# A dense layer folded into one on-chip matrix per batch, and run in one block with the SwiGLU

## The reference

```python
x = x + attention(x, ...)       # 8 key heads of 4 query heads each, paged cache of 512 keys + 128 new ones
# the dense layer, with W (512, 512), b (512), coeff (8), mask (8, 512, 512) of 0 or 1
output = einsum('bsi,oi->bso', x, W) + b
sign   = 2 * mask - 1
diff   = einsum('bsi,bio->bso', x, sign)
x = x + output + diff * coeff[:, None, None]
x = x + swiglu(x, ...)          # W_gate, W_up (1376, 512), W_down, each with a rank-16 adapter picked by batch
x = x + einsum('bsi,boi->bso', x, L3_weight[ids])
```

## Time and profile before

| | |
|---|---|
| median of 3 runs | 1438.1 us (1436.93 to 1439.56) |
| profiled execution, its own time | 1439.11 us |
| its span, first to last instruction | 1437.3 us |
| TensorE busy | 1386.7 us, 96% of the span |
| VectorE busy | 986.5 us, 69% |
| ScalarE busy | 852.8 us, 59% |
| GpSimd busy | 675.3 us, 47% |
| granted TensorE clock, mean | 0.992 |
| moved by DMA | 163.93 MB |

### The profile page before, as it was taken

How to read it: one execution, slowest core, us unless ns; L and a number is a source line. 1 busy time by engine, 2 the same in 40 slices (tenths; PEclk the granted TensorE clock), 3 DMA queues, 4 the chain that set the end, 5 groups by cost and what they waited for, 6 DMA issues and landing times. The chain is left out here.

```text
span 1437.3 us, 25483 instructions
## 1 busy us (share of the span) xinstructions
PE 1386.7 (96%) x7864; PEld 1206.7 (84%) x7864; DVE 986.5 (69%) x2067; ACT 852.8 (59%) x2200; POOL 675.3 (47%) x965
## 2 busy tenths in 40 slices
PE   5999999999999999999999999999998869999998
PEld 4888888888888888888888888888887657888886
DVE  6777777777777777777777777777775645545544
ACT  6666665766576556666665666666554636434444
POOL 5765565555555555655565555555443550000202
PEclk9999999999999999999999999999999989999999
DMA  5354236414621462155236413621210553533422
GB/s 181 109 173 144 59 89 194 126 33 125 203 66 29 146 204 58 44 166 155 58 88 191 117 42 120 203 70 31 38 51 1 192 169 106 173 135 113 167 87 103
DMA packets 162395, 163.93 MB, mean 114 GB/s; under 512 B 121632, under 2 KB 129440, under 8 KB 152096
## 3 DMA queue, kind: packets, MB, share of 16 engines
q1 hardware_dynamic: 156384, 127.54, 30.0%
q0 software_dynamic: 5952, 35.65, 7.5%
HBM read 131.71 MB, written 31.46 MB: 114 GB/s over the span
## 5 line engine op out<-in xcount | busy, mean ns | idle before, releaser
L496 ACT ACTIVATE at_pT_hi<-at_ps 128x512 fp32r<-128x512 f32 x320 | 178.4, 600 | 173.6 <-PE at_ps L884 173.4
L422 POOL TENSOR_SCALAR at_probs<-at_probs,at_row_inv 128x640 f32<-128x640 f32 x256 | 205.6, 803 | 155.3 <-DVE at_row_inv L716 147.0
L661 DVE TENSOR_TENSOR at_pT_lo<-at_ps,at_pT_hi 128x512 fp32r<-128x512 f32 x320 | 208.5, 685 | 91.6 <-ACT at_pT_hi L496 91.6
L710 DVE CUSTOM_DVE_ANT_0 at_scores<-at_ps,at_mask,at_inv_rms 128x640 f32<-128x640 f32 x256 | 224.1, 878 | 67.9 <-PE at_ps L65 66.4
L539 ACT ACTIVATE at_probs<-at_scores,at_neg_max 128x640 f32<-128x640 f32 x256 | 213.1, 833 | 57.9 <-DVE at_neg_max L710 56.5
L63 PE MATMUL at_ps<-at_kT_hi,at_qT_hi 128*128 128x320 f32 x512 | 164.8, 322 | 0.3 <-DVE at_qT_lo L661 0.2
L884 PE MATMUL at_ps<-ident,at_probs 128*128 128x128 f32 x1280 | 160.5, 272 | 1.7 <-POOL at_probs L422 1.7
L65 PE MATMUL at_ps<-at_kT_hi,at_qT_lo 128*128 128x320 f32 x512 | 158.2, 309 | 0.0
L64 PE MATMUL at_ps<-at_kT_lo,at_qT_hi 128*128 128x320 f32 x512 | 158.0, 309 | 0.0
L884 PEld LDWEIGHTS at_ps<-ident,at_probs 128*128 128x128 f32 x1280 | 145.0, 141 | 10.8 <-POOL at_probs L422 2.4
L63 PE MATMUL at_ps<-at_pT_hi,at_v_hi 128*128 128x512 f32 x320 | 131.8, 412 | 2.1 <-DVE at_pT_lo L661 2.1
(11 more groups left out here) (211 smaller groups left out, 3496.6 us busy)
## 6 DMA issues: line engine op xcount, KB each, us to landing
kT_pages<-at_kv_stage SPq DMA_DIRECT2D x14, 1024.0 KB, 4.6
v_pages<-at_kv_stage SPq DMA_DIRECT2D x14, 1024.0 KB, 4.5
at_k_raw<-kT_pages SPq DMA_DIRECT2D x56, 256.0 KB, 3.2
at_v_raw<-v_pages SPq DMA_DIRECT2D x56, 256.0 KB, 3.9
sw_wgu_raw<-in_sw_gu SPq DMA_DIRECT2D x22, 512.0 KB, 3.3
staging<-in_L_cond_Wq SPq DMA_DIRECT2D x8, 1024.0 KB, 6.8
staging<-in_L_cond_Wo SPq DMA_DIRECT2D x8, 1024.0 KB, 5.1
ds_mask_raw<-in_mask_Bx4096x_ik SPq DMA_DIRECT2D x8, 1024.0 KB, 5.2
```

What stands on the lines that cost most here:

```text
L422: pool.tensor_scalar(probs[:, h, :], probs[:, h, :], row_inv[:, h:h + 1], 1.0, ALU.mult, ALU.mult).then_inc(probs_done, 1)
L496: act.activation(out, src, ACT.Copy).then_inc(done, 1)
L661: dve.tensor_tensor(out, src, hi_part.bitcast(F32), ALU.subtract).then_inc(done, 1)
L710: dve.tensor_tensor_reduce(out=scores[h % 2][:], in0=slot(h), in1=mask[:, b, :], scale=inv_rms[b % 2][:, h:h + 1], scalar=3.0e38, op0=ALU. ...
```

## The change

The dense layer is done with one matrix per batch, M = W^T + I + 2 coeff mask, in float32. W comes turned from the host; GpSimd adds the identity to `staging` once (`prepare_dense`); VectorE makes a quarter of a matrix per instruction, in place of the mask (`DenseWeights.weights`), ScalarE makes its high part, GpSimd three of the four rests (two for batch 0) and VectorE the others. Then there are 12 products per batch. VectorE adds the bias and a per-token term, which ScalarE gets as a row sum of -coeff x.

The dense block and the SwiGLU block are one (`dense_swiglu`), unrolled. Batches 0 to 3 are turned for the SwiGLU between dense products; the rank products stand ahead of the last dense product. Three 1 MB tiles, `shared`, hold masks; they are also kv_stage, the tables of cosines and sines in attention, and later bd_raw, ad_raw, acts and y. Mask 0 and W are loaded in attention's last group, masks 1 and 2 behind the last use of the tables. Batch 0's four quarters are made by VectorE at the end of steps 4, 5 and 6 of the last group (one, one, two), the first two of batch 1 ahead of the last `attended`. All eight register reads of adapter numbers stand in attention's queue of SP, behind its last key and value loads.

```diff
@@ -323,6 +323,12 @@
             def group(g, last):
                 for b in range(B):
                     g2, b2 = following(*following(g, b))
+                    if last and b == 0:
+                        sp.wait_ge(kv_stored, (HK - 1) * 64)
+                        dense.load_mask(sp, 0)
+                    if last and b == 2:
+                        sp.wait_ge(wo_done, HK * WO_GROUPS)
+                        sp.dma_start(wq_raw[:], dense.w).then_inc(dense.w_loaded, 16)
@@ -346,8 +352,12 @@
...
             group(HK - 1, True)
-            sp.wait_ge(wo_done, HK * WO_GROUPS)
-            sp.dma_start(wq_raw[:], dense_w.rearrange("(c p) i -> p c i", p=P)).then_inc(dense_w_staged, 16)
+            loads.pick(sp, 0)
+            loads.pick(sp, 1)
+            sp.wait_ge(q_turned, HK * B)
+            sp.wait_ge(k_turned, HK * B)
+            dense.load_mask(sp, 1)
+            dense.load_mask(sp, 2)
@@ -475,6 +485,17 @@
...
+                    if last and b == 3:
+                        prepare_dense()
+            def prepare_dense():
+                pool.tensor_scalar(dense.coeff2[:], coeff_sb, 2.0, 1.0, ALU.mult, ALU.mult).then_inc(dense.ready, 1)
+                pool.tensor_scalar(dense.minus_coeff[:], coeff_sb, -1.0, 1.0, ALU.mult, ALU.mult).then_inc(dense.ready, 1)
+                pool.wait_ge(dense.w_loaded, 16)
+                for c in range(DC):
+                    at = wq_raw[:, c, c * P:(c + 1) * P]
+                    pool.tensor_tensor(at, at, ident[:], ALU.add).then_inc(dense.ready, 1)
@@ -806,11 +827,16 @@
...
+                    if last:
+                        for c in {4: (0,), 5: (1,), 6: (2, 3)}.get(b, ()):
+                            dense.weights(dve, 0, c)
...
             group(HK - 1, False, True)
+            dense.weights(dve, 1, 0)
+            dense.weights(dve, 1, 1)
             attended(HK, 0)
...
+class DenseWeights:
...
+    def rows(self, b):
+        return self.masks[b % 3][:].rearrange("p (c n) -> p c n", c=DC)
+    def load_mask(self, eng, b):
+        eng.dma_start(self.rows(b).bitcast(I32), self.mask[b].rearrange("(c p) n -> p c n", p=P)).then_inc(self.mask_loaded[b % 3], 16)
+    def weights(self, dve, b, c):
+        if b == 0 and c == 0:
+            dve.wait_ge(self.ready, 2 + DC)
+        if c == 0:
+            dve.wait_ge(self.mask_loaded[b % 3], b // 3 * 16 + 16)
+        at = self.rows(b)[:, c, :]
+        dve.scalar_tensor_tensor(out=at, in0=at.bitcast(I32), scalar=self.coeff2[:, b:b + 1], in1=self.staged[:, c, :],
+                                 op0=ALU.mult, op1=ALU.add).then_inc(self.done, 1)
...
-        acts = [sb(f"acts{j}", [P, NTOK]) for j in range(2)]
+        acts = [shared[0][:, j * NTOK:(j + 1) * NTOK] for j in range(2)]
...
         w3_lo = [sb(f"w3_lo{j}", [P, DC, DM], F32R) for j in range(2)]
-        y = [sb(f"y{j}", [P, DM]) for j in range(2)]
+        y = [shared[0][:, 2 * NTOK + j * DM:2 * NTOK + (j + 1) * DM] for j in range(2)]
...
+        dense_hi, dense_lo, x1_hi, x1_lo = w3_hi, w3_lo, acts_hi, acts_lo
+        sums_junk = [(x_hi, x_lo)[b // QUAD][1][:, b % QUAD, :] for b in range(B)]
+        POOL_LO = [(0, 2)] + [(0, 2, 3)] * (B - 1)
+        X1_BANK, DENSE_BANK = [6, 7], [0, 1]
@@ -1369,10 +1212,35 @@
...
-            loads.pick(sp, 1)
+            def mask_read(b):
...
+                sp.wait_ge(dense_lo_pool_done, lo_count(b, POOL_LO[b][-1]))
+                sp.wait_ge(dense_lo_dve_done, lo_count(b, max(c for c in range(DC) if not on_pool(b, c))))
...
+            def next_mask(b):
+                mask_read(b - 3)
+                dense.load_mask(sp, b)
+            sp.dma_start(bias_sb[:], bias.rearrange("(o d) -> o d", o=1).broadcast_to([P, DM])).then_inc(bias_loaded, 16)
+            sp.dma_start(sel[:], sel_in).then_inc(sel_loaded, 16)
+            loads.a_ranks(sp, 0)
+            next_mask(3)
+            loads.weights(sp, 0)
+            loads.b_ranks(sp, 0)
+            next_mask(4)
+            loads.down_ranks(sp, 0)
+            loads.weights(sp, 1)
+            next_mask(5)
+            loads.b_ranks(sp, 1)
+            next_mask(6)
+            loads.weights(sp, 2)
+            next_mask(7)
+            loads.b_ranks(sp, 2)
+            mask_read(5)
+            loads.down_b_ranks(sp, 0)
+            loads.down_ranks(sp, 1)
@@ -1408,6 +1277,14 @@
...
+            def dense_part(b, c):
+                pool.wait_ge(dense_hi_done, b * DC + c + 1)
+                pool.tensor_tensor(dense_lo[b % 2][:, c, :], dense.rows(b)[:, c, :], dense_hi[b % 2][:, c, :].bitcast(F32),
+                                   ALU.subtract).then_inc(dense_lo_pool_done, 1)
+            for b in range(B):
+                for c in POOL_LO[b]:
+                    dense_part(b, c)
@@ -1508,19 +1385,54 @@
...
+            def dense_part(b, c):
+                act.wait_ge(dense.done, b * DC + c + 1)
+                if b >= 2:
+                    act.wait_ge(dense_in_psum, b - 1)
+                hi(dense_hi[b % 2][:, c, :], dense.rows(b)[:, c, :], dense_hi_done)
...
+            def row_sums(b):
+                act.activation(sums_junk[b], xres[:, b, :], ACT.Identity, scale=dense.minus_coeff[:, b:b + 1],
+                               accum_out=sign_bias[:, b:b + 1]).then_inc(sums_done, 1)
...
+            dense_part(0, 0)
+            x1_turned(0)
+            for c in range(1, DC):
+                dense_part(0, c)
+            row_sums(0)
+            x1_turned(1)
+            for b in range(B):
+                if b + 1 < B:
+                    for c in range(DC):
+                        dense_part(b + 1, c)
+                    row_sums(b + 1)
+                if b + 2 < B:
+                    x1_turned(b + 2)
+                if 1 <= b <= QUAD:
+                    tokens(b - 1, DOWN + b - 1)
+                if b == 1:
+                    gate_up_a(0)
+                if b == 4:
+                    gate_up_weights(0)
+                    act.activation(ident_r[:], ident[:], ACT.Copy)
+                if b == 5:
+                    zero_rows()
             ranks(0, SIDE)
             b_columns(0)
@@ -1629,14 +1541,46 @@
...
+            def dense_part(b, c):
+                lo(dense_lo[b % 2][:, c, :], dense.rows(b)[:, c, :], dense_hi[b % 2][:, c, :], dense_hi_done, b * DC + c + 1, dense_lo_dve_done)
...
+            def add_dense(b):
+                dve.wait_ge(bias_loaded, 16)
+                dve.wait_ge(sums_done, b + 1)
+                dve.wait_ge(dense_in_psum, b + 1)
+                dve.scalar_tensor_tensor(out=xres[:, b, :], in0=ps[:, DENSE_BANK[b % 2], :], scalar=sign_bias[:, b:b + 1], in1=bias_sb[:],
+                                         op0=ALU.add, op1=ALU.add).then_inc(x2_done, 1)
+            x1_turned(0)
+            dense_part(0, 1)
+            dense_part(0, 3)
+            dense.weights(dve, 1, 2)
+            dense.weights(dve, 1, 3)
+            x1_turned(1)
+            for b in range(B):
+                if b + 1 < B:
+                    dense_part(b + 1, 1)
+                if b + 2 < B:
+                    for c in range(DC):
+                        dense.weights(dve, b + 2, c)
+                if b < B - 1:
+                    add_dense(b)
+                if b + 2 < B:
+                    x1_turned(b + 2)
+                if 1 <= b <= QUAD:
+                    tokens(b - 1, DOWN + b - 1)
+                if b == 1:
+                    gate_up_a(0)
+                if b == 4:
+                    gate_up_weights(0)
             dve.wait_ge(sel_loaded, 16)
             ranks(0, SIDE)
             b_columns(0)
             ranks(1, TD)
+            add_dense(B - 1)
@@ -1675,6 +1619,7 @@
...
+                pe.wait_ge(x2_done, b + 1)
...
+                if n < 2:
+                    pe.wait_ge(x1_done, B - n)
...
+                pe.wait_ge(x2_done, B - 1)
...
             def up(n):
+                pe.wait_ge(x2_done, B)
...
-            for b in range(QUAD):
-                tokens(b, DOWN + b)
-            ranks(0, SIDE)
-            ranks(1, TD)
...
+            def dense_product(b):
+                j = b % 2
+                pe.wait_ge(x1_done, b + 1)
+                if b >= 2:
+                    pe.wait_ge(x2_done, b - 1)
+                for c in range(DC):
+                    pe.wait_ge(dense_lo_pool_done if on_pool(b, c) else dense_lo_dve_done, lo_count(b, c))
+                    at = slice(c * S, (c + 1) * S)
+                    ins = three_pass(pe, ps[:, DENSE_BANK[j], :], x1_hi[j][:, at], x1_lo[j][:, at], dense_hi[j][:, c, :], dense_lo[j][:, c, :], c == 0, c == DC - 1)
+                ins.then_inc(dense_in_psum, 1)
+            x1_turn(0)
+            x1_turn(1)
+            for b in range(B):
+                dense_product(b)
+                if b + 2 < B:
+                    x1_turn(b + 2)
+                if 1 <= b <= QUAD:
+                    tokens(b - 1, DOWN + b - 1)
+                if b == B - 2:
+                    ranks(0, SIDE)
```

(33 more changed lines are left out.)

282 lines of the change are left out of this document (44 added, 238 removed).

## The result

The changed kernel takes 1413.87 us (median of 4 runs, 1413.40 to 1414.49) against 1437.84 (1436.93 to 1439.56) for the kernel before: ratio 0.9832, 95% interval 0.9815 to 0.9849. It is 24.0 us faster; 20.1 were forecast (1438.1 less 1418.0). The profiled execution took 1413.4 us, its span is 1411.5, against 1437.3.

What follows compares the result with a forecast made beforehand. New bound: a port shared by VectorE and GpSimd, making dense block's start to first up product (the distance) 62 instead of 81.6 us. Span 1437.3 + 1.1 - 19.6 - 1.6 = 1417.2, median 1418.0; own range 1411 to 1425.

Steps and rivals of the forecast that it cites:

- What bounded the kernel before: Dense block to first up product, 81.6 us: TensorE bounds, except 11.2 us idle, mostly from SP's 9.05 us of register reads.
- What is removed; TensorE alone would need 31 us: Dense stage: 96 of 192 products, 16 transposes, the block boundary and most of the head go; TensorE's remainder is 31 us.
- The new bound, 52.9 us of a shared port, last rest at 55: Dense stage: VectorE and GpSimd exclude each other, their times adding to 52.9 us, 6.8 per batch; last rest at 55.
- Standstills 1.5, then last product and gate: Dense stage's end: 1.5 us when both engines wait, then 1.9 of the last dense product and 3.1 of gate; sum 60.
- The clock, +2: TensorE's half clock in much of the dense stage shows at its end, +2 us; behind the first up product, -1.6.
- Attention +1.1: Attention's last group: VectorE's quarters at b = 4 and 5 delay GpSimd's rotation of q, 2 x 0.55 us; bounds 0 to +3.
- Loads hidden with 5 to spare: Dense stage's masks: three periods, 20.5 us, cover 15.5 of landing and path to the last rest, 5 us to spare.
- (a): Rival: half clock all through the dense stage, gate and up included, giving 1423 us; chance 0.15.
- (b): Rival: the shared port doesn't bind, short instructions slip past each other, 15 us less, 1403; chance 0.09.
- (c): Rival: dense masks land late, 15 us to landing, two rounds losing 5 us each, 1428; chance 0.06.
- (d): Rival: a GpSimd rest costs 3.06 us whenever VectorE runs, +41 us, 1459, slower than before; chance 0.05.
- (e): Rival: mask 1 comes late, batch 1 isn't ready at the block's start, up to 5 us lost, 1423; chance 0.05.

Runs made afterwards that it cites:

- before_picks: Kernel before the change, with only the two sets of SP register reads moved from the dense block to attention's end of SP's queue: 1428.46 us, ratio 0.9934.
- twice: Changed kernel with the dense products of all eight batches computed a second time over the first, same output: 1417.62 us, ratio 0.9857 to the kernel before.
- rest4: Changed kernel with all four rests of every batch on GpSimd, 32 instead of 23: 1419.36 us, ratio 0.9866 to the kernel before.
- gu_late: Changed kernel with VectorE's gate/up rest moved from ahead of batch 6's rest to behind batch 7's: 1411.49 us, ratio 0.9817 to the kernel before.
- warm: Changed kernel with the dense products of batches 0 to 5 computed twice, same output: 1414.22 us, ratio 0.9838 to the kernel before.
- late_picks: Changed kernel with the register reads put back into the dense block's part of SP's queue: 1414.06 us, ratio 0.9835 to the kernel before.

## Why the prediction was right, and where sizes were off

Its span was 1417.2; 1411.5 were measured. The 5.7 us between are: start-up of the execution 2.05, attention 0.27, distance 3.4, the rest to the end 0.0. By the medians it is 4.1. Of the signs that it named, the sets of 12 products per 6.5 to 7.5 us and the 240 to 242 us behind the up product came; the first up product at 60 to 65 us was missed, 58.6.

**What bounded the kernel before.** Right. before_picks shows SP's register reads as what held 7.8 us of the distance; 2.5 of the idleness stay at the boundary without them.

**What is removed; TensorE alone would need 31 us.** Right that it doesn't set the time: 22 us more of it cost 3.2 (twice).

**The new bound, 52.9 us of a shared port, last rest at 55.** The mechanism, mutual exclusion, holds (rest4; the kinds of 0.68 and 1.28 lengthened). The term came near by number, and in part by luck: the bound it was made into is the wrong one. Two things took its place. First, the three PSUM operations of VectorE, which the prediction put under it without a price, run beside GpSimd's rests for nothing, and a GpSimd rest amid quarters costs VectorE 1.04, not 1.27: of three rests a batch it paid for 1.5 us. Second, VectorE's queue is what never idles: 5.1 of its own and 1.5 of waits make 6.6, where the port's sum said 6.8. The quarter goes at 0.66, not 0.60, and takes 0.74 alone; the 0.69 doesn't follow from the slope given with it (2.29 less three times 0.60 is 0.49). GpSimd's rests took 1.52 in the mean, where the signs named 1.9, and its last ended at 51.2 instead of 55.

**Standstills 1.5, then last product and gate.** GpSimd stood 4.35 us behind the zero rows, more than forecast, but off the path: the last dense product started at 1165.23, 1.7 behind the last rest. The end was set by VectorE's queue up to batch 7's x rest (48.25, with TensorE's slow products of batch 6 up to 48.39), which the sum doesn't have, and then by TensorE: rank products 4.5, last dense product 2.8, gate 2.9. gu_late, warm and the 9.7 us common to the variants show it. At full clock this way is 57.9 us long (48.25 + 9.7), where the sum said 60: 2.1 of the 3.4 by which the distance missed.

**The clock, +2.** This term is mis-sized; it is 0.7. The half clock came, 0.84 of full speed over the stage. In the end stretch nine products took 4.0 us instead of some 2.2, but these 1.8 were hidden behind VectorE's x rest (warm); only the rank products' 0.6 and 0.1 of the nine reached the end. That is the other 1.3 of the 3.4. The 1.6 behind the up product came exactly, 240.57 for 242.18. A part of that is luck: both of these profiles have the half clock near their end, which is worth one microsecond and is missing in six others (last section).

**Attention +1.1.** Right in place and kind, 0.83 in size: some 0.44 each, not 0.55. The additions on GpSimd cost nothing, mask 1 was early.

**Loads hidden with 5 to spare.** Right: late_picks puts the slack of mask 3 at 6.

**The rivals.** (a), half clock throughout: no, it was 0.84, and full from the last dense product on. (b), no binding port: refuted by rest4 and the lengthened kinds. (c), late masks: 6.4 us to landing, not 15. (d), 3.06 a rest: 1.52 in the mean. (e), mask 1 late: no.

## What to carry to other kernels

When two engines can block each other, write out the queue of the busier one with its waits in it, and mark which of its operations can be blocked at all; a sum over the shared resource hides both the free overlap and the queue. Moving work to the blocking engine pays only as far as it fits beside the unblockable operations: here one rest of four, not three and not none. Price a slow stretch only after asking what else ends there: nine products at half clock cost next to nothing, as another engine's operation ended with them. And look at a serial queue of slow commands in front of a boundary before rewriting what is around it: moving two lines gave the old kernel 40% of what the whole change gave.

## What the runs showed of the hardware that was not expected

- VectorE with a PSUM input next to a working GpSimd kept its 0.67 to 0.74 us, and GpSimd its 1.28; the same line of code with two SBUF inputs took 1.04 in the mean. The Trainium skill, "SBUF — State Buffer", section "SBUF: two separate sides", ties the exclusion to the ports that VectorE uses with two SBUF inputs, and these rows agree.
- The clock behind one and the same wait can go either way. Near the end TensorE waits 2.3 us for VectorE's sw_x_lo in both of these rows, table by stretch, kernel after and then kernel late_picks, the same stretch of the program:

```profile
1390.90:1400.90 10.00, 7.71 (x32) 6.27 (x31) 7.35 (x6) 6.71 (x9) 2.74 (x6) 0.83 0.35 131
```
```profile
1392.40:1402.40 10.00, 7.72 (x39) 6.37 (x38) 7.31 (x7) 7.29 (x9) 4.82 (x6) 1.00 0.37 140
```

  Of the fourteen profiles here, eight have the half clock there and six don't. Behind the first up product the eight take 240.6 to 240.7 us (the kernel before 1.6 more, for its other cold stretch), the six 239.5 to 239.7, with the same work. One microsecond between two profiles can be no more than this, and start-up another two.
